# An expert loop with its gathers dealt one per expert, split TensorE signals, and routed rows collected in parts

## The chip, the cores and the metric

The kernel runs on one core of a Trainium2 chip. The metric is device time in microseconds (us), from one launch of the whole program. Engines are called by their profile names: PE is TensorE, ACT ScalarE, DVE VectorE, POOL GpSimd, SP the queue that issues most DMAs.

## What is computed

Four blocks in a row, each with a residual and a layer norm, on 2048 tokens of 128 values in fp32:

- causal linear attention with 16 heads of 8;
- a mixture of experts: a shared expert for all tokens, and 64 experts of width 384, of which each token takes its best 8 (weights renormalised over those 8);
- four encoder layers (linear attention, then a relu block of width 512), after `x * sqrt(128) + positions`;
- a routed block: the 75% of tokens with the highest scores go through `gelu(x @ w_block)`.

```python
h = jnp.einsum('ech,efh->ecf', buf, expert_w1)      # buf: each expert's tokens
x1, x2 = jnp.split(h, 2, axis=-1)
out = jnp.einsum('ecf,ehf->ech', x1 * jax.nn.silu(x2), expert_w2)
y = out[se, rank] * sw[:, None]                      # its gate
combined = jnp.zeros((T, H), x.dtype).at[st].add(y)
return shared_out + combined
```

## The kernel before

Five hand-ordered instruction streams, one for each engine, meet only in counting semaphores; no planner orders anything.

**Routing.** After the first attention the rows of x1 and the gates go to DRAM (`dispatch_rows`, 768 B a row). Experts are handled in 16 quads `Q` of `EG = 4`, experts `n = 4Q + j`. A quad has 5 blocks `b` of 128 slots, 160 slots for each of its experts. One-hot tables (`R["a"]`, `R["b"]`) multiplied on PE give the slot lists `gather_all` and `scatter_all`.

**The expert loop.** For expert `n` PE does: `expert_result(n - 2)` (L790, 3 products), then for `j` = 0 `turn_results(Q - 2, 1)`, for 1 and 2 `turn_inputs(Q + 1, j - 1)`, for 3 `turn_results(Q - 1, 0)` (the transposes L774 and L760), then `expert_hidden(n)` (L780, 6 products), which alone increments `expert_mm`. Each fp32 product has two matmul records. On `expert_mm >= n + 1` wait:

- ACT: `silu_of(n)` (L1153), then `keep_result(n - 2)` (L1157);
- DVE: `rows_back` (L1754) or `columns_of` (L1731), then `product(n)` (L1743), which also waits for the silu and which `expert_result(n)` waits for;
- SP: the next load of weights into a ring of 8 (576 KB an expert, L455);
- POOL: `step(n)`, its indirect DMAs. A gather (L1340) fetches 128 routed rows, a scatter (L1347) writes 128 weighted results to `returned_rows`. 30 gathers are issued ahead; then for each quad, from `n = 4Q + 8` on, at its four steps: 2 scatters, 3 scatters, 2 gathers, 3 gathers. The gathered rows have `GOT = 4` buffers.

**The way back.** When the last of 80 scatters has landed, SP reads `returned_rows` in 16 tiles of 512 KB (L467), in four groups `g` of 4 tiles. Meanwhile PE, ACT and DVE finish the shared expert of groups 2 and 3 (`late_hidden` L830 and L831, `late_product` L1791, `late_rows` L838, `add_base` L1787), all of it ahead of DVE's `collect`. `collect(g)` waits for all 4 tiles of its group; each tile is summed over its 8 rows per token in three halvings. `SUMMED = (3, 2, 0, 0)` is the number of tiles of each group that DVE sums (L1816, L1818); the others are POOL's (`sum_tiles`, L1469). Then the shared expert's rows are added (L1822), the norm taken (its rstd on POOL, L271), and `begin_state(0)`, `norm1` and the first layer's `turn_norm1` (L857) follow, one after the other.

Of the kernel before, what the change touches and what calls it, by code (L numbers as in the profile page):

```python
# [115 lines left out]
def program(nc, cst, xt0, xr0, l0w, l0p, l0r, bo0, l0s, ew, l1w, l1p, l1r, fin_r, mod_w, out):  # L116
    with ExitStack() as ctx:
# [27 lines left out]
        def carve(parts, at=0):  # L145

            made = {}
            for name, shape, dt in parts:
# [7 lines left out]
                elif len(shape) == 3:  # L156
# [48 lines left out]
        R = carve([("a", (TILES, NEG * RA * EG), F16), ("b", (2 * RB, TE), F16), ("mask", (TE,), F16)])  # L205
# [120 lines left out]
        SUMMED = (3, 2, 0, 0)  # L326
# [96 lines left out]
        def _(sp):  # L423
            sp.dma_start(w0[:, 0:W_O], l0w[:, 0:W_O]).then_inc(sem("first_in"), 16)
            sp.dma_start(cols(xt, 0), cols(xt0, 0)).then_inc(sem("first_in"), 16)
            sp.dma_start(l0ps[:], l0p).then_inc(sem("l0p_in"), 16)
            sp.dma_start(kv_bias[:], l0r.partition_broadcast(P)).then_inc(sem("l0p_in"), 16)
            sp.dma_start(C[:, 0:C_BLK], cst[:, 0:C_BLK]).then_inc(sem("first_consts_in"), 16)
            sp.dma_start(cols(xt, 1), cols(xt0, 1)).then_inc(sem("second_xt_in"), 16)
            sp.dma_start(w0[:, W_O:], l0w[:, W_O:]).then_inc(sem("wo_in"), 16)  # L430
            sp.dma_start(xr[:], xr0).then_inc(sem("xr_in"), 16)
            sp.dma_start(xt[:, 2 * GROUP:], xt0[:, 2 * GROUP:]).then_inc(sem("xt_in"), 16)
            sp.dma_start(sw[:], l0s).then_inc(sem("sw_in"), 16)
# [23 lines left out]
            sp.wait_ge(sem("expert_mm"), NE + LAG)  # L457
            sp.dma_start(w_qkv, l1w[0][:, 0:3 * P]).then_inc(sem("qkv_in"), 16)
            sp.dma_start(layer_cols[:], l1p).then_inc(sem("cols_in"), 16)
            sp.dma_start(lrows, l1r.rearrange("l a d -> l (a d)").partition_broadcast(P)).then_inc(sem("rows_in"), 16)  # L460
            sp.dma_start(w_o, l1w[0][:, 3 * P:4 * P]).then_inc(sem("o_in"), 16)
# [4 lines left out]
            for i in range(TILES):  # L466
                sp.dma_start(spare[i], mine[i]).then_inc(sem(f"returned_in{i // GT}"), 16)  # L467
            sp.dma_start(w_up, l1w[0][:, 4 * P:8 * P]).then_inc(sem("up_in"), 16)
            sp.dma_start(w_down, l1w[0][:, 8 * P:12 * P]).then_inc(sem("down_in"), 16)
            sp.dma_start(mod_sb, mod_w).then_inc(sem("mod_in"), 16)  # L470
            sp.dma_start(fin_rows, fin_r.rearrange("a d -> (a d)").partition_broadcast(P)).then_inc(sem("fin_in"), 16)

            with sp.Fori(1, LAYERS) as l:
                w = l1w[bass.ds(l, 1)].rearrange("a p n -> (a p) n")
                sp.wait_ge(sem("kv1_mm"), 2 * GROUPS * l)
                sp.dma_start(w_qkv, w[:, 0:3 * P]).then_inc(sem("qkv_in"), 16)
                sp.wait_ge(sem("out1_mm"), GROUPS * l)
                sp.dma_start(w_o, w[:, 3 * P:4 * P]).then_inc(sem("o_in"), 16)
                sp.wait_ge(sem("up_mm"), FFB * GROUPS * l)
                sp.dma_start(w_up, w[:, 4 * P:8 * P]).then_inc(sem("up_in"), 16)  # L480
                sp.wait_ge(sem("down_mm"), GROUPS * l)
                sp.dma_start(w_down, w[:, 8 * P:12 * P]).then_inc(sem("down_in"), 16)
# [6 lines left out]
        def _(pe):  # L489
# [4 lines left out]
            def project_first(g):  # L494
                if g == 1:
                    pe.wait_ge(sem("second_xt_in"), 16)
                if g == 2:
                    pe.wait_ge(sem("xt_in"), 16)
# [6 lines left out]
                pe.matmul(bank[0][:], w0[:, W_Q:W_Q + P], cols(xt, g), start=True, stop=True).then_inc(sem("q_mm"), 1)  # L505
# [82 lines left out]
            def attention_out(g, to):  # L588
                if g == 0:
                    pe.wait_ge(sem("wo_in"), 16)  # L590
# [22 lines left out]
            def route_logits(g):  # L613
                if g == 0:
                    pe.wait_ge(sem("sw_in"), 16)
# [106 lines left out]
            a16 = R["a"].rearrange("p i (g n) -> p i g n", n=RA * EG)  # L722
            b16 = R["b"].rearrange("p b (i e) -> p b i e", e=NE)

            def find_slots(call):
# [4 lines left out]
                for k, q in enumerate(FOUND[call]):  # L730
                    pe.wait_ge(sem("one_hots_ready"), 2 * q + 2)
                    for u in range(2):
                        at = 2 * RB * EG * (2 * k + u)
                        lo = EG * (2 * q + u)
                        for i in range(TILES):
                            mm = pe.matmul(slot_bank(call)[:, at:at + 2 * RB * EG], a16[:, i, 2 * q + u, :],
# [75 lines left out]
            turn_results(NEG - 2, 1).then_inc(sem("expert_mm"), 1)  # L812
            expert_result(NE - 1).then_inc(sem("expert_mm"), 1)
# [52 lines left out]
            def project(n, k, g, l):  # L866
                pe.wait_ge(sem("qkv_in"), 16 * (l + 1))
# [36 lines left out]
            def output(n, k, g, l):  # L904
                pe.wait_ge(sem("o_in"), 16 * (l + 1))
# [18 lines left out]
            def up(n, k, g, l):  # L924
                pe.wait_ge(sem("up_in"), 16 * (l + 1))
# [11 lines left out]
            def down(n, k, g, l):  # L937
                pe.wait_ge(sem("down_in"), 16 * (l + 1))
# [21 lines left out]
            def score(g):  # L960
                if g == 0:
                    pe.wait_ge(sem("mod_in"), 16)
                    pe.wait_ge(sem("mid_ready"), ITEMS)
                else:
# [3 lines left out]
                    sem("score_mm"), 1)  # L968
# [68 lines left out]
        def _(act):  # L1037
            def parts_of_q(g):
                act.wait_ge(sem("q_mm"), g + 1)
# [60 lines left out]
            act.wait_ge(sem("l0p_in"), 32)  # L1100
# [121 lines left out]
            def keep_scores(g):  # L1222
                if g >= 2:
                    act.wait_ge(sem("chosen"), g - 1)
                act.wait_ge(sem("score_mm"), g + 1)
# [66 lines left out]
        def _(pool):  # L1292
# [16 lines left out]
            def add_bias(g):  # L1309
                if g == 0:  # L1310
                    pool.wait_ge(sem("xr_in"), 16)
# [40 lines left out]
            AHEAD = 6  # L1352
# [725 lines left out]
```

## Time and profile before

| | us |
|---|---|
| median of 3 runs | 721.71 |
| lowest, highest | 721.12, 726.26 |
| the profiled execution | 723.01 |
| its span, first to last instruction | 721.2 |
| mean granted TensorE clock | 0.919 |

The profile is of one execution; times in it count from its first instruction. A row `start, us, engine line op out<-in xcount [idle <- releaser]` says that the engine sat idle that long before it, and what released it. Matmul ends are modelled. Idle time of an engine that is not the bottleneck costs nothing.

### The profile page before, as it was taken

Reading aid. Unit: us, or ns where it says so; the run is one execution under the profiler, and the core shown is the slowest. Engines: PE = TensorE matmul, PEld = TensorE weight load, DVE = VectorE, ACT = ScalarE, POOL = GpSimd, SP = SyncE. Lnnn points to the kernel's source line nnn. Section 1 sums busy time; section 2 is a strip of 40 time slices with the busy share of each in tenths; the row PEclk is TensorE's granted clock in tenths of the full one; section 3 lists DMA queues with packets and bytes.
Section 4 is the critical chain, followed back from the end, with each engine's and each line's share of the span. In section 5 each row is a group of like instructions: output and inputs, shape, how many; then the busy total and the mean of one; then the engine's idle time right before and its main releaser. Section 6 shows DMA issues by size and latency. Waiting matters only on the chain.

```text
span 721.2 us, 11097 instructions
## 1 busy us (share of the span) xinstructions
PE 580.0 (80%) x3755; PEld 479.8 (67%) x3755; DVE 453.1 (63%) x1362; ACT 230.2 (32%) x434; POOL 345.1 (48%) x341
## 2 busy tenths in 40 slices
PE   7998878668987787797999035789999999999960
PEld 5767655668977776797995024567787778778640
DVE  4678768943424322333433787887877787777994
ACT  3142234002322212222332011224344444443664
POOL 4656101873566666576444488343322332342352
PEclk9999997879999999999999556799999999999995
DMA  8960001126666766676716900000000000000001
GB/s 298 415 260 23 16 7 36 45 72 203 209 222 200 231 220 190 190 237 218 239 61 213 398 2 0 0 12 5 15 26 4 15 15 11 4 30 0 1 1 59
DMA packets 29564, 79.42 MB, mean 110 GB/s; under 512 B 7104, under 2 KB 12096, under 8 KB 29264
## 3 DMA queue, kind: packets, MB, share of 16 engines
q1 hardware_dynamic: 23088, 65.69, 26.3%
q0 software_dynamic: 6432, 13.16, 6.0%
q8 instruction: 25, 0.41, 0.2%
q14 instruction: 19, 0.16, 0.1%
HBM read 62.60 MB, written 16.25 MB: 109 GB/s over the span
## 4 chain that ended last, share of the span: by engine, by line
PE 58%; DVE 23%; issue 8%; another core or an unknown queue 4%; POOL 2%; ACT 2%; DMA 1%; SPq 0%; DVEq 0%; ACTq 0%; POOLq 0%
PE bank L780 13%; PE bank L946 6%; PE bank L790 6%; PE bank L934 6%; PE bank L539 4%; PE bank L876 3%; PE bank L894 2%; DVE stats L256 2%; DVE arena L1659 2%; PE bank L857 2%; PE bank L871 2%; DVE hidden L1743 2%; PE bank L885 2%; PE bank L912 2%
## 5 line engine op out<-in xcount | busy, mean ns | idle before, releaser
L271 POOL TENSOR_TENSOR rstd<-veps,minus_half 128x4 f32<-128x4 f32 x52 | 54.0, 1039 | 209.9 <-DVE veps L264 208.4
L780 PE MATMUL bank<-hidden,ring 128*128 128x160 f32 x768 | 123.4, 311 | 4.6 <-issue 2.7
L780 PEld LDWEIGHTS bank<-hidden,ring 128*128 128x128 f32 x768 | 113.4, 200 | 6.5 <-issue 4.3
L1347 POOL DMA_INDIRECT returned_rows<-x1t,scatter_all x80 | 79.3, 991 | 65.9 <-DVE x1t L1754 21.8
L1153 ACT ACTIVATE hidden<-bank 128x480 f32<-128x480 f32 x64 | 36.9, 576 | 177.6 <-PE bank L780 110.5
L790 PE MATMUL bank<-hidden,ring 128*128 128x160 f32 x384 | 66.4, 310 | 31.8 <-DVE hidden L1743 19.1
L790 PEld LDWEIGHTS bank<-hidden,ring 128*128 128x128 f32 x384 | 56.0, 193 | 37.3 <-DVE hidden L1743 22.8
L1731 DVE COPY hidden<-bank 128x384 f32<-128x384 f32 (+1 forms) x32 | 22.9, 719 | 66.3 <-PE bank L780 33.9
L1211 ACT ACTIVATE arena<-bank,layer_cols 128x512 f32<-128x512 f32 x64 | 44.0, 687 | 62.6 <-PE bank L934 62.6
L946 PE MATMUL bank<-ring,arena 128*128 128x128 f32 x512 | 59.9, 275 | 1.4 <-issue 1.4
L946 PEld LDWEIGHTS bank<-ring,arena 128*128 128x128 f32 x512 | 58.4, 192 | 2.4 <-issue 2.4
L1754 DVE TENSOR_TENSOR x1t<-bank,slot_gate 128x384 f32<-128x384 f32 (+1 forms) x32 | 15.6, 490 | 68.2 <-PE bank L780 52.6
L934 PE MATMUL bank<-arena,ring 128*128 128x512 f32 x128 | 57.6, 592 | 0.0
L857 PE MATMUL bank<-consts,arena 128*128 128x128 f32 x192 | 28.8, 285 | 26.3 <-DVE arena L295 26.2
L1743 DVE TENSOR_TENSOR hidden<-bank,hidden 128x480 f32<-128x480 f32 x64 | 41.7, 652 | 13.1 <-ACT hidden L1153 7.5
L295 DVE TENSOR_SCALAR arena<-shared,mv,rstd 128x128 f32<-128x128 f32 x128 | 38.1, 361 | 7.8 <-POOL rstd L271 7.8
L857 PEld LDWEIGHTS bank<-consts,arena 128*128 128x128 f32 x192 | 22.9, 145 | 29.9 <-DVE arena L295 24.0
L934 PEld LDWEIGHTS bank<-arena,ring 128*128 128x128 f32 x128 | 23.2, 190 | 23.4 <-issue 23.3
L1307 POOL TENSOR_TENSOR arena<-arena 128x512 f32<-128x512 f32 x30 | 32.7, 1122 | 12.5 <-DVE arena L1504 12.5
L539 PEld LDWEIGHTS bank<-consts,arena 128*128 128x128 f32 x256 | 31.8, 200 | 7.5 <-issue 4.2
L1513 DVE TENSOR_TENSOR arena<-bank,arena 128x512 f32<-128x512 f32 x36 | 24.4, 685 | 18.1 <-PE bank L539 12.2
L876 PEld LDWEIGHTS bank<-ring,arena 128*128 128x128 f32 x128 | 26.9, 210 | 13.0 <-issue 9.9
(222 smaller groups left out, 1156.9 us busy)
## 6 DMA issues: line engine op xcount, KB each, us to landing
ring<-in_ew SPq DMA_DIRECT2D x64, 576.0 KB
returned_rows<-zeros SPq DMA_DIRECT2D x16, 512.0 KB, 14.6
arena<-returned_rows SPq DMA_DIRECT2D x6, 512.0 KB, 12.7
hidden<-returned_rows SPq DMA_DIRECT2D x4, 512.0 KB, 5.0
ring<-returned_rows SPq DMA_DIRECT2D x4, 512.0 KB, 8.6
ring<-in_l1w SPq DMA_DIRECT2D x8, 256.0 KB, 2.6
returned_rows<-x1t,scatter_all POOLq DMA_INDIRECT x80
shared<-in_xr SPq DMA_DIRECT2D x1, 1024.0 KB, 8.3
```

Of the source, the lines that this page charges most:

```text
L271: pool.tensor_tensor(rstd[:, s, :], veps[:, s, :], minus_half[:], ALU.pow).then_inc(sem(f"rstd{which}_ready"), 1)
L295: ins = v.tensor_scalar(dst[:, i, :], src[:, i, :], mv[:, s, i, 0:1], rstd[:, s, i:i + 1], ALU.subtract, ALU.mult)
L539: mm = pe.matmul(bank[3 + c % 3][:, tile_of(t)], A["kvp"][:, g % 2, t, P * e:P * e + P], cum, start=True, stop=True)
L780: mm = pe.matmul(bank[2 * (n % 2) + part][:, CAP * f:CAP * f + CAP], ring[:, n % RING, P * (FB * part + f):P * (FB * part + f) + P], E["xt ...
L790: mm = pe.matmul(bank[4 + n % 2][:, 0:CAP], ring[:, n % RING, P * (2 * FB + f):P * (2 * FB + f) + P], E["prod"][:, n % 2, CAP * f:CAP * f ...
L857: mm = pe.transpose(bank[b][:, P * t:P * t + P], src[:, t, :], ident)
L876: mm = pe.matmul(bank[3 + h][:, 2 * D * t:2 * D * t + 2 * D], B["ht"][:, g, P * (2 * h + t):P * (2 * h + t) + P], w_qkv[:, P:3 * P], start ...
L934: pe.matmul(bank[(3, 4, 6, 7)[f]][:], w_up[:, P * f:P * f + P], B["ht"][:, g], start=True, stop=True).then_inc(sem("up_mm"), 1)
L946: mm = pe.matmul(bank[5][:, P * t:P * t + P], B["relu"][:, g % 2, f, P * t:P * t + P], w_down[:, P * f:P * f + P], start=(f == 0), stop=(f ...
L1211: act.activation(B["relu"][:, g % 2, f], bank[(3, 4, 6, 7)[f]][:], ACT.Relu, bias=layer_col(l, 5 + f)).then_inc(sem("relu_ready"), 1)
L1347: pool.indirect_dma_start(returned_dram[:, :], bass.IndirectOffsetOnAxis(ap=scatter_all[:, Q, b:b + 1], axis=0), E["back"][:, Q % BACK, b, ...
L1743: v.tensor_tensor(E["prod"][:, n % 2, :], bank[2 * (n % 2)][:, 0:FB * CAP], E["silu"][:, n % 2, :], ALU.mult).then_inc(sem("prod_g_ready"), 1)
```

## The change

Four things, and a renaming of semaphores (one serves first one transfer and later another, with the counts raised to match; PE's `project` waits for `16 * (l + 2)` instead of `16 * (l + 1)`, and so on) that frees some for new uses.

1. **Gathers and scatters.** The one-hot table `R["a"]` is laid out by quads, so that its first four quads become four more gather buffers (`GOT = 8`). 20 gathers are issued ahead of the loop, then 2 for each of experts 0 to 7, then 1 for each expert to 51; the scatters of a quad go 1, 1, 2, 1.
2. **Two signals.** PE increments `rows_mm` after `expert_result(n - 2)` and the turn, ahead of `expert_hidden(n)`; `expert_mm` stays behind `expert_hidden(n)`. ACT keeps result `n - 2` on `rows_mm`, ahead of its silu; DVE copies on `rows_mm` and multiplies when the silu is there.
3. **Return in parts.** DVE sums all of group 0 (`SUMMED = (4, 2, 0, 0)`), in parts of 2, 1 and 1 tiles, each when it has landed; POOL sums none of it.
4. **Later bases.** DVE's last two late products come behind its wait for the scatters, `add_base(2)` behind `collect(0)`, `add_base(3)` behind `norm_stats` of the first layer's norm; PE's first projection waits for both.

```diff
-        R = carve([("a", (TILES, NEG * RA * EG), F16), ...
+        R = carve([("a", (NEG, TILES, RA * EG), F16), ...
-        GOT, BACK = 4, 3
+        GOT, BACK = 8, 3
+        got_at += [arena[:, TILES * RA * EG // 2 * q:TILES * RA * EG // 2 * q + RB * ROUTED] for q in range(GOT - 4)]
...
-        SUMMED = (3, 2, 0, 0)
+        SUMMED = (4, 2, 0, 0)
+        PARTS = ((0, 2), (2, 1), (3, 1))
+
+        def returned_in(i):
+            return sem(f"returned_part{(0, 0, 1, 2)[i]}") if i < GT else sem(f"returned_in{i // GT}")
...
-            sp.wait_ge(sem("expert_mm"), NE + LAG)
+            sp.wait_ge(sem("rows_mm"), NE + LAG - 1)
...
             for n in range(NE):
                 Q, j = n // EG, n % EG
                 if n >= LAG:
-                    expert_result(n - LAG)
+                    done = expert_result(n - LAG)
+                if j == 0 and Q >= 2:
+                    done = turn_results(Q - 2, 1)
+                elif j in (1, 2) and Q < NEG - 1:
+                    done = turn_inputs(Q + 1, j - 1)
+                elif j == 3 and Q >= 1:
+                    done = turn_results(Q - 1, 0)
+                if n:
+                    done.then_inc(sem("rows_mm"), 1)
                 if j == 0:
-                    if Q >= 2:
-                        turn_results(Q - 2, 1)
                     pe.wait_ge(sem("xt_read"), 2 * (Q + 1))
-                elif j < 3 and Q < NEG - 1:
-                    turn_inputs(Q + 1, j - 1)
-                elif j == 3 and Q >= 1:
-                    turn_results(Q - 1, 0)
...
             def project(n, k, g, l):
+                if k == 0:
+                    pe.wait_ge(sem("base_ready"), GROUPS)
...
             for n in range(NE + LAG):
-                act.wait_ge(sem("expert_mm"), n + 1)
+                if n >= LAG:
+                    act.wait_ge(sem("rows_mm"), n)
+                    keep_result(n - LAG)
                 if n < NE:
+                    act.wait_ge(sem("expert_mm"), n + 1)
                     silu_of(n)
-                if n >= LAG:
-                    keep_result(n - LAG)
...
-            AHEAD = 6
+            BEFORE, FIRST_SCATTER = 4, 2 * EG
...
+            gather_blocks(0, BEFORE * RB)
             pool.wait_ge(sem("zeroed"), 16 * TOK * TOPK // (8 * P))
+            for n in range(NE + LAG):
+                if n < NE:
+                    pool.wait_ge(sem("expert_mm"), n + 1)
+                else:
+                    pool.wait_ge(sem("rows_mm"), n)
+                if n < FIRST_SCATTER:
+                    gather_blocks(BEFORE * RB + 2 * n, 2)
+                else:
+                    Q = (n - FIRST_SCATTER) // EG
+                    gathering = BEFORE * RB + FIRST_SCATTER + n < NEG * RB
+                    for b in (((0,), (1,), (2, 3), (4,)) if gathering else ((0, 1), (2, 3), (4,), ()))[n % EG]:
+                        scatter_block(Q, b)
+                    gather_blocks(BEFORE * RB + FIRST_SCATTER + n, 1)
...
             for n in range(NE):
                 Q, j = n // EG, n % EG
-                v.wait_ge(sem("expert_mm"), n + 1)
+                if n:
+                    v.wait_ge(sem("rows_mm"), n)
...
             def collect(g):
-                v.wait_ge(sem(f"returned_in{g}"), 16 * GT)
-                count = SUMMED[g]
...
+                if g == 0:
+                    for first, count in PARTS:
+                        v.wait_ge(returned_in(first), 16 * count)
+                        k = add_rows(g, first, count)
```

## Rows read from the trace of the kernel before

**Rows 1.** Busy time by stretch: expert loop (three), scatters' end, first layers.

```profile
152.00:184.00 32.00, 27.41 (x173) 26.65 (x174) 10.33 (x23) 7.35 (x16) 14.25 (x16) 0.87 0.52 161
184.00:334.00 150.00, 121.84 (x834) 116.02 (x833) 49.74 (x101) 36.07 (x81) 97.76 (x101) 0.97 0.66 213
343.00:376.00 33.00, 32.41 (x244) 32.18 (x242) 14.48 (x28) 11.69 (x26) 14.73 (x15) 1.00 0.50 157
404.00:476.00 72.00, 34.64 (x131) 25.97 (x132) 58.50 (x173) 13.05 (x18) 47.03 (x48) 0.67 0.15 58
```

**Rows 2.** Timeline, two neighbouring experts late in the loop.

```profile
356.81 1.80 PE L780 MATMUL bank<-hidden,ring 128*128 128x160 f32 x12
358.65 0.57 ACT L1153 ACTIVATE hidden<-bank 128x480 f32<-128x480 f32 x1 [1.85 <-PE bank L780]
359.48 1.80 PE L780 MATMUL bank<-hidden,ring 128*128 128x160 f32 x12
```

**Rows 3.** Timeline, one quad of the middle, in order of time.

```profile
277.28 0.82 DVE L1731 COPY hidden<-bank 128x384 f32<-128x384 f32 x1 [3.18 <-PE bank L780]
277.95 0.64 DVE L1743 TENSOR_TENSOR hidden<-bank,hidden 128x480 f32<-128x480 f32 x1
278.02 0.98 POOL L1347 DMA_INDIRECT returned_rows<-x1t,scatter_all  x1 [2.08 <-PE bank L780]
279.30 0.98 POOL L1347 DMA_INDIRECT returned_rows<-x1t,scatter_all  x1 [0.30 <-issue]
282.56 1.80 PE L780 MATMUL bank<-hidden,ring 128*128 128x160 f32 x12
285.33 1.80 PE L780 MATMUL bank<-hidden,ring 128*128 128x160 f32 x12
286.97 0.95 POOL L1340 DMA_INDIRECT arena<-dispatch_rows,gather_all  x1 [0.30 <-issue]
288.04 0.57 ACT L1153 ACTIVATE hidden<-bank 128x480 f32<-128x480 f32 x1 [5.39 <-PE bank L780]
288.64 0.66 DVE L1743 TENSOR_TENSOR hidden<-bank,hidden 128x480 f32<-128x480 f32 x1 [0.18 <-issue]
288.81 1.01 POOL L1347 DMA_INDIRECT returned_rows<-x1t,scatter_all  x1 [0.90 <-PE bank L780]
289.36 1.27 PE L790 MATMUL bank<-hidden,ring 128*128 128x160 f32 x6 [2.23 <-issue]
292.49 0.57 ACT L1153 ACTIVATE hidden<-bank 128x480 f32<-128x480 f32 x1 [3.53 <-remote]
293.23 0.98 POOL L1347 DMA_INDIRECT returned_rows<-x1t,scatter_all  x1 [2.10 <-remote]
```

**Rows 4.** Timeline of POOL, start of the loop.

```profile
173.94 0.94 POOL L1340 DMA_INDIRECT logits<-dispatch_rows,gather_all  x1 [0.30 <-issue]
184.03 1.02 POOL L1347 DMA_INDIRECT returned_rows<-x1t,scatter_all  x1 [9.15 <-DVE x1t L1754]
```

**Rows 5.** Timeline, from the last scatter to the first norm of the sum.

```profile
387.98 0.98 POOL L1347 DMA_INDIRECT returned_rows<-x1t,scatter_all  x1 [0.30 <-issue]
390.24 1.76 SPq L467 DMA_DIRECT2D hidden<-returned_rows  x4
397.27 0.69 DVE L1787 TENSOR_TENSOR shared<-bank,x 128x512 f32<-128x512 f32 x1 [3.04 <-PE bank L838]
398.00 3.72 POOL L1469 TENSOR_TENSOR hidden<-hidden 128x512 f32<-128x512 f32 x2 [9.04 <-DMA hidden<-returned_rows]
403.30 0.69 DVE L1822 TENSOR_TENSOR arena<-arena,shared 128x512 f32<-128x512 f32 x1
406.78 1.12 DVE L295 TENSOR_SCALAR x<-arena,mv,rstd 128x128 f32<-128x128 f32 x4 [1.15 <-POOL rstd L271]
```

**Rows 6.** The tile hidden from 376 to 400 us: DVE's first halving, and the landings.

```profile
L1816 DVE TENSOR_TENSOR hidden<-hidden x1: 2697/2697/2697, 398.4 to 398.4; 128x1536 f32<-128x1536 f32 x1
DMA to landing us min/median/max: 3.6/5.0/6.3
```

More of the change, by code:

```diff
@@ L504, in project_first @@
                     pe.wait_ge(sem("logits_ready"), g - 2)
-                pe.matmul(bank[0][:], w0[:, W_Q:W_Q + P], cols(xt, g), start=True, stop=True).then_inc(sem("q_mm"), 1)
+                pe.matmul(bank[0][:], w0[:, W_Q:W_Q + P], cols(xt, g), start=True, stop=True).then_inc(sem("q_mm_then_score_mm"), 1)
                 for h in range(2):
@@ L811, in _ @@
             expert_result(NE - 2)
[L812 to L813 removed]
+            turn_results(NEG - 2, 1).then_inc(sem("rows_mm"), 1)
+            expert_result(NE - 1).then_inc(sem("rows_mm"), 1)
             for c in range(2):
@@ L1350, in scatter_block, with gather_blocks @@
                                         oob_is_err=False).then_inc(sem(f"scattered{Q % BACK}"), 16)
[L1352 removed]
+            BEFORE, FIRST_SCATTER = 4, 2 * EG
+            def gather_blocks(first, count):
+                for k in range(first, min(first + count, NEG * RB)):
+                    gather_block(k // RB, k % RB)
             pool.wait_ge(sem("rows_out"), 16 * 2 * GROUPS)
[L1354 to L1356 removed]
+            gather_blocks(0, BEFORE * RB)
             pool.wait_ge(sem("zeroed"), 16 * TOK * TOPK // (8 * P))
[L1358 to L1375 removed]
+            for n in range(NE + LAG):
[11 more added lines that the diff above has]
+                    gather_blocks(BEFORE * RB + FIRST_SCATTER + n, 1)
+            scatter_block(NEG - 2, RB - 1)
+            for b in range(RB):
+                scatter_block(NEG - 1, b)
             def row_of(l, k):
@@ L1459, in sum_tiles @@
             def sum_tiles(g):
+                if SUMMED[g] == GT:
+                    return
                 pool.wait_ge(sem(f"returned_in{g}"), 16 * GT)
@@ L1658, in low_table @@
                 n = last - first
-                ins = v.tensor_tensor(a_out[:, first:last, Q],
+                ins = v.tensor_tensor(a_out[:, Q, first:last],
                                       a_in[:, first:last, EG * Q:EG * Q + EG].unsqueeze(2).to_broadcast([P, n, RA, EG]),
@@ L1773, in _ @@
                     gates_of(Q + 1)
-            v.wait_ge(sem("expert_mm"), NE + 1)
+            v.wait_ge(sem("rows_mm"), NE)
             rows_back(NEG - 2, 1)
@@ L1797, in _ @@
                 late_product(m)
-            add_base(SOON)
-            for m in range(FB * SOON + 4, FB * GROUPS):
-                late_product(m)
-            add_base(SOON + 1)
             v.wait_ge(sem("consts_in"), 16)
@@ L1808, in _, with add_rows @@
             blk = C[:, C_BLK:C_BLK + P]
-            def collect(g):
-                v.wait_ge(sem(f"returned_in{g}"), 16 * GT)
-                count = SUMMED[g]
-                if count:
-                    rows = spare_rows(g, 0, count)
-                    for width in (4 * D, 2 * D):
-                        ch.after(ch.did(v.tensor_tensor(rows[:, :, 0:width], rows[:, :, 0:width],
-                                                        rows[:, :, width:2 * width], ALU.add)))
-                    k = ch.did(v.tensor_tensor(H[:, g, 0:count, :], rows[:, :, 0:D], rows[:, :, D:2 * D], ALU.add))
+            def add_rows(g, first, count):
+                rows = spare_rows(g, first, count)
+                for width in (4 * D, 2 * D):
+                    ch.after(ch.did(v.tensor_tensor(rows[:, :, 0:width], rows[:, :, 0:width],
+                                                    rows[:, :, width:2 * width], ALU.add)))
+                return ch.did(v.tensor_tensor(H[:, g, first:first + count, :], rows[:, :, 0:D], rows[:, :, D:2 * D], ALU.add))
+            def collect(g):
+                if g == 0:
+                    for first, count in PARTS:
+                        v.wait_ge(returned_in(first), 16 * count)
+                        k = add_rows(g, first, count)
+                else:
+                    v.wait_ge(sem(f"returned_in{g}"), 16 * GT)
+                    if SUMMED[g]:
+                        k = add_rows(g, 0, SUMMED[g])
+                if SUMMED[g]:
                     ch.after(k)
-                v.wait_ge(sem("pool_sums"), 3 * sum(GT - n for n in SUMMED[:g + 1]))
+                if SUMMED[g] < GT:
+                    v.wait_ge(sem("pool_sums"), 3 * sum(GT - n for n in SUMMED[:g + 1]))
                 v.wait_ge(sem("base_ready"), g + 1)
@@ L2021, in _ @@
             ch.after(ch.did(v.tensor_scalar(lrows[:, :, 0:D], lrows[:, :, 0:D], 1.0, None, ALU.add)))
+            for m in range(FB * SOON + 4, FB * GROUPS):
+                late_product(m)
             steps = GROUPS * (2 * 2 * GT + 1 + 3)
```

102 lines of the change are left out of this document (43 added, 59 removed).

## The prediction

> **What bounds the kernel now.** I read the busy time by stretch first. Late in the expert loop, 343 to 376 us, PE is busy 32.4 of 33 us; in the middle, 184 to 334 us, 121.8 of 150 [rows 1]. An expert has 18 matmul records of its own and on average 2.5 transposes, 20.5 in all. So the late stretch does 244/20.5 = 11.9 experts at 2.77 us each, which is PE's own pace, and the middle 834/20.5 = 40.7 experts at 3.69 us. That is 0.92 us an expert that PE does not need, 37 us over the middle, in a loop that everything after it waits for.
>
> Then the timeline, to see what PE waits for. In the late stretch the silu starts at 358.65, when the products of 356.81 + 1.80 have just ended [rows 2]. In the middle it does not. The products of 282.56 end by their records at 284.36, and ACT starts its silu at 288.04, 3.7 us late; those of 285.33 end at 287.13 and the silu starts at 292.49, 5.4 us late [rows 3]. DVE, SP and POOL, which wait for the same `expert_mm`, start with ACT to within 0.1 us where they have nothing else to wait for: POOL's wait of 2.10 us ends at 293.23, behind that same signal and its set-up. The count arrives late. PE then sits idle 2.23 us before the result product at 289.36 [rows 3].
>
> What stands beside it is POOL. From 278.02 to 293.23 it issues the quad's 10 indirect DMAs, 1.29 us from one start to the next (279.30 less 278.02), and the two pauses in that time exceed the usual 0.30 by 0.6 and 1.8 us [rows 3]: 12.9 + 2.4 = 15.3 us for four experts, of which PE needs 11.1. In the late stretch POOL has 15 such DMAs in 33 us and no gathers, and the signals come on time [rows 1, 2]. So the loop's middle goes at POOL's pace, by way of signals that come late while POOL issues without a break. Why a signal is held is not in the trace.
>
> Last the way back. The last scatter is issued at 387.98, SP reads from 390.24 on, the fourth tile lands at 397.9 and DVE's addition of the base starts at 403.30 [rows 5, 6]. Nothing of the first layer can start before it.
>
> **Gathers and scatters.** The change does not take a DMA away; it moves them. From expert 8 to 51 POOL now has 44 gathers and 55 scatters, 9 for four experts instead of 10. Before, 101 of POOL's instructions in 150 us took 101 x 1.29 = 130.3 us, and 19.7 us were pauses, for ten quads 2.0 us each [rows 1, 3]. After, eleven quads take 99 x 1.29 = 127.7 us, and if pauses stay at 2.0 us a quad, 21.7 more: 149.4 us. Before, the same 44 experts took 40.7 in 150 us and 3.3 at 2.77: 159.1 us. The difference is **-9.7 us**, the term I take for this part. Its bounds are far apart. From below: all signals on time, PE at 2.77 us, 44 x 2.77 = 121.9 us, -37. From above: a pause after every expert, 9 x 1.29 + 4 x 1.2 = 16.4 us a quad (1.2 is half of the 2.4 above), 180.5 us, +21. I take the middle value since it is the same rule, 10 DMAs and two pauses, read on 9.
>
> Experts 0 to 7: before, 173/20.5 = 8.4 experts took 32 us, 8.7 more than at 2.77 [rows 1]; POOL finished its 30 gathers at 174.9 and then sat idle for 9.15 us [rows 4], in which the signals were on time. After, it issues 2 x 1.25 us in every 2.77 us and that rest is gone, but so are the five in a row. I take 0, with -7 and +5 as bounds (the excess gone; five clean experts at the middle's 0.92 us more). Gathers run 28 blocks ahead of the expert number and are needed at 5 blocks a quad, so the last, issued at expert 51, is needed at 57: no wait of PE for rows. Scatters of a quad are all out by n = 4Q + 11, and DVE needs the buffer again at 4Q + 19.
>
> The table's new layout has the same elements in each instruction; 0, and the find-slots products read the same 128 columns.
>
> **Two signals.** When a signal comes late, DVE copies 384 columns for 0.82 us ahead of the product, and the product starts 0.67 us behind the copy's start; where the copy is the shorter one it starts 0.60 us behind, which is the silu's 0.57 [rows 3]. With the copy done during the hidden products, 0.07 to 0.15 us are saved at each expert whose product PE waits for, some 15 in the middle: **-1.0**, bounds -3 and 0. Where PE never waits this is worth nothing. What is queued behind ACT's new wait is the silu; ACT waits for the count of a turn that is ahead of the hidden products on PE, so it cannot be the later of the two. The 63 added increments I price at 0, since the product that carries them is not lengthened in any row; but they are 63 more signals of the kind that come late, and that belongs to the slow rival.
>
> A rule speaks against this part. The Trainium skill, in TensorE: Matmul & The Clock Gate, under the cost of the per-tile semaphore tail, says that increments serialize, with a fit of 26.3 ns each; as an estimate from that page, 65 of them would add 1.7 us. No row here shows the cost of one, and the sum does without it.
>
> **Return in parts.** SP's first read is issued at 390.24; the landings take 3.6 us for the first and 6.3 for the fourth, which was issued last, at about 391.6 [rows 5, 6]. So tiles land near 393.9, 395.3, 396.6 and 397.9. DVE used to start at 398.4 with 1536 columns, for 2.70 us; 512 columns take 0.69 us elsewhere (L1822), so 1536 should take 3 x 0.53 + 0.16 = 1.75 [rows 5, 6]. POOL was summing beside it for 3.72 us [rows 5], and now it does not. Part 0 takes 1.23 + 0.69 + 0.42 and gaps, 2.4 us, from 395.3 to 397.7; parts 1 and 2 take 0.69 + 0.42 + 0.29 + 0.1 = 1.5 each, to 399.2 and 400.7. The addition of the base then starts at 400.8 instead of 403.30: **-2.5**, bounds 0 (each step at the slower rate of 2.70/1.75, part 2 done at 403.0) and -3.5. On this the skill agrees with the row: SBUF — State Buffer, under who interferes with whom, says that a DVE instruction with two SBUF inputs contends with a GpSimd instruction that reads SBUF.
>
> The moved work: `late_product` 10 and 11 are behind the wait for the scatters, which ends near 390.3, and their silus come later than that anyway; before, DVE's last base addition ran at 397.27, only 0.4 us ahead of the collecting [rows 5]. It and its twin now take 0.69 us each in DVE's waits for a rstd, of which the first is 1.15 us long [rows 5], and the second alike. If that cover were gone they would cost 1.4 us. PE's new wait for the bases is behind `h1_ready`, which comes later on DVE. The first layers, 404 to 476 us, are DVE's (58.5 of 72 us busy [rows 1]) and shift as a whole.
>
> **The sum.** -9.7 - 1.0 - 2.5 = -13.2. The profiled execution took 723.0 us, 1.3 above the median, so 709.8 on its scale and **708.5** on the median's. A difference of 1%, 7.2 us, is about what the measurement of this kernel can tell from none.
>
> **The rivals.**
> - Signals on time throughout (0.22). Gathers no longer come five in a row, and scatters alone in runs of five hardly delay a signal [rows 2]. Then -37 and up to -7 for the loop and -2.5: between 675 and 685. Against it: POOL still issues 9 x 1.29 = 11.6 us in PE's 11.1, without a break.
> - The deal changes nothing (0.20): each gather costs what it costs, wherever it stands. Then only the return's 2.5 and the copy's 1.0: 718.
> - More pauses, slower (0.15). A late signal is let through when POOL has run out of permitted work; with a small portion at each step, POOL runs out at every expert, and each time all engines wait. At x pauses of 1.2 us a quad costs 11.6 + 1.2x; it breaks even with 14.5 at x = 2.4, and at four the loop loses 21 us: 723 + 21 - 3.5 - 1.3 = 739. The two signals for each expert speak for it, the on-time signals of the late stretch, with five scatters in a run, against.
> - The forecast (0.43), 700 to 716 by its own bounds.
>
> **Range and chances.** 680 takes in most of the first rival, 729 the milder half of the slow one; outside are the strongest forms of both. Faster by over 1%: 0.36 + 0.22 + 0.04 = 0.62. Within: 0.05 + 0.16 + 0.03 = 0.24. Slower: 0.14.
>
> **What would show it.** Right: 184 to 334 us holds about 900 matmul records instead of 834, POOL's DMAs still 1.29 us apart, fewer waits over 3 us of ACT for L780, base addition some 2.5 us closer to the last scatter. Wrong: as many late silus per quad as before (second rival), one late silu for each expert and POOL pauses near 2 us after every step (third), or no late silu and PE busy over 95% (first). A DVE wait for the second base, or PE waiting for gathered rows, would break terms that I set to 0.

## The result and the profile after

| us | before | after |
|---|---|---|
| median (4 runs each) | 721.41 | 711.5 |
| span of the profiled execution | 721.2 | 709.9 |
| mean granted TensorE clock | 0.919 | 0.920 |

The ratio is 0.9843, 95% interval 0.9801 to 0.9886: 1.6% faster. By the two spans the change took 11.3 us off. First the busy time by stretch of the kernel after, the same stretches as [rows 1].

```profile
152.00:184.00 32.00, 28.50 (x186) 27.73 (x186) 10.18 (x23) 7.96 (x17) 19.68 (x21) 0.89 0.55 179
184.00:334.00 150.00, 128.51 (x896) 124.06 (x895) 55.48 (x112) 42.22 (x89) 97.54 (x98) 0.97 0.69 226
343.00:376.00 33.00, 30.69 (x199) 26.91 (x200) 14.30 (x28) 11.58 (x24) 17.89 (x18) 1.00 0.47 147
404.00:476.00 72.00, 43.51 (x202) 33.06 (x201) 59.89 (x172) 17.66 (x25) 44.39 (x48) 0.76 0.03 11
```

The middle, 184 to 334 us, holds 896 matmul records where before had 834, and 98 POOL instructions where it had 101: more experts for about as many DMAs. To see where the 11.3 us lie I take both traces apart at events that both have: the first product of experts 0, 8 and 52, the last scatter, the first product of the first layer (PE's `turn_norm1`) and the end.

```
us                                before    after   difference
to the start of expert 0          152.97   153.16     +0.2
experts 0 to 7                     28.38    26.50     -1.9
experts 8 to 51                   161.81   151.06    -10.8
expert 52 to the last scatter      44.82    48.20     +3.4
last scatter to turn_norm1         24.88    22.23     -2.7
turn_norm1 to the end             308.34   308.73     +0.4
```

Next the timeline of the kernel after, one quad of the middle, to hold against [rows 3].

```profile
288.05 0.99 POOL L1358 DMA_INDIRECT returned_rows<-x1t,scatter_all  x1 [0.30 <-issue]
289.34 0.99 POOL L1351 DMA_INDIRECT arena<-dispatch_rows,gather_all  x1 [0.30 <-issue]
289.61 1.80 PE L786 MATMUL bank<-hidden,ring 128*128 128x160 f32 x12
290.63 1.01 POOL L1358 DMA_INDIRECT returned_rows<-x1t,scatter_all  x1 [0.30 <-issue]
291.94 0.99 POOL L1351 DMA_INDIRECT arena<-dispatch_rows,gather_all  x1 [0.30 <-issue]
294.31 0.57 ACT L1163 ACTIVATE hidden<-bank 128x480 f32<-128x480 f32 x1 [0.38 <-remote]
294.91 0.66 DVE L1757 TENSOR_TENSOR hidden<-bank,hidden 128x480 f32<-128x480 f32 x1 [1.02 <-ACT hidden L1163]
295.05 1.00 POOL L1358 DMA_INDIRECT returned_rows<-x1t,scatter_all  x1 [2.12 <-PE bank L786]
295.62 1.08 PE L796 MATMUL bank<-hidden,ring 128*128 128x160 f32 x6 [1.02 <-DVE hidden L1757]
```

The signals still come late: the products of 289.61 end by their records at 291.41, and ACT's silu starts at 294.31, 2.9 us late. POOL still issues at 1.29 to 1.31 us and then stands for 2.12 us. Of the 44 experts 22 have a silu over 1 us late, 24 before. What has changed is the number of DMAs: 98 from the start of expert 8 to that of expert 52, where before has 105, with pauses that add up to about as much.

The 3.4 us that were given back lie where before had no late signals at all. The last gather now goes out at expert 53 (expert 49 in before), and POOL issues from 329.0 to 340.6 almost without a break, nine DMAs, of which these are the last six:

```profile
332.91 1.01 POOL L1358 DMA_INDIRECT returned_rows<-x1t,scatter_all  x1 [0.30 <-issue]
334.22 0.99 POOL L1351 DMA_INDIRECT arena<-dispatch_rows,gather_all  x1 [0.30 <-issue]
335.51 1.00 POOL L1358 DMA_INDIRECT returned_rows<-x1t,scatter_all  x1 [0.30 <-issue]
336.17 1.80 PE L786 MATMUL bank<-hidden,ring 128*128 128x160 f32 x12
336.82 0.99 POOL L1358 DMA_INDIRECT returned_rows<-x1t,scatter_all  x1 [0.30 <-issue]
338.37 0.98 POOL L1358 DMA_INDIRECT returned_rows<-x1t,scatter_all  x1 [0.56 <-issue]
338.94 1.08 PE L796 MATMUL bank<-hidden,ring 128*128 128x160 f32 x6 [0.98 <-issue]
339.65 0.98 POOL L1358 DMA_INDIRECT returned_rows<-x1t,scatter_all  x1 [0.30 <-issue]
342.21 0.61 ACT L1163 ACTIVATE hidden<-bank 128x480 f32<-128x480 f32 x1
343.57 1.08 PE L796 MATMUL bank<-hidden,ring 128*128 128x160 f32 x6 [1.08 <-DVE hidden L1757]
```

The silu of the products that end at 337.97 starts at 342.21, 4.2 us late. Experts 54 and 55 take 4.03 and 4.52 us here, where before takes 2.77 and 2.67. From expert 52 on, up to its wait ahead of the last result product, PE stands idle for 2.3 us in all, and in before not at all.

Last the way back, the timeline of the kernel after against [rows 5], and the landings from the tile `hidden` against [rows 6].

```profile
378.92 0.98 POOL L1358 DMA_INDIRECT returned_rows<-x1t,scatter_all  x1 [0.30 <-issue]
386.25 1.95 DVE L1824 TENSOR_TENSOR hidden<-hidden 128x1024 f32<-128x1024 f32 x2 [1.07 <-DMA hidden<-returned_rows]
388.23 0.43 DVE L1826 TENSOR_TENSOR arena<-hidden 128x256 f32<-128x256 f32 x1
391.47 0.69 DVE L1842 TENSOR_TENSOR arena<-arena,shared 128x512 f32<-128x512 f32 x1
393.70 0.68 DVE L1802 TENSOR_TENSOR shared<-bank,x 128x512 f32<-128x512 f32 x1
395.31 1.11 DVE L296 TENSOR_SCALAR x<-arena,mv,rstd 128x128 f32<-128x128 f32 x4 [0.93 <-POOL rstd L272]
DMA to landing us min/median/max: 3.8/5.4/7.0
```

From the last scatter to the addition of the base it takes 391.47 - 378.92 = 12.55 us, where before took 15.32. The moved `add_base` (L1802) runs at 393.70 and DVE still waits 0.93 us for the rstd behind it.

### The profile page after: what moved, and what is told of

The parts are those of the page before. It is cut to its first block, busy times and chain, and to the rows that moved or that the text cites. A ratio compares the mean times of both kernels' runs of the same rounds, so it can differ in the third digit from the quotient of the medians.

```text
span 709.9 us, 11093 instructions
## 1 busy us (share of the span) xinstructions
PE 576.3 (81%) x3755; PEld 478.2 (67%) x3755; DVE 453.5 (64%) x1368; ACT 233.6 (33%) x434; POOL 342.1 (48%) x338
## 4 chain that ended last, share of the span: by engine, by line
PE 58%; DVE 19%; issue 10%; another core or an unknown queue 5%; ACT 3%; POOL 3%; DMA 1%; SPq 0%; DVEq 0%; ACTq 0%; POOLq 0%
PE bank L786 11%; PE bank L956 7%; PE bank L796 6%; PE bank L944 6%; PE bank L545 4%; PE bank L886 3%; PE bank L904 2%; DVE stats L257 2%; PE bank L865 2%; ACT hidden L1163 2%; PE bank L879 2%; DVE hidden L1757 2%; PE bank L895 2%; PE bank L922 2%
## 5 line engine op out<-in xcount | busy, mean ns | idle before, releaser
L786 PE MATMUL bank<-hidden,ring 128*128 128x160 f32 x768 | 121.5, 309 | 3.4 <-DVE hidden L1745 2.5
L796 PE MATMUL bank<-hidden,ring 128*128 128x160 f32 x384 | 66.4, 310 | 26.2 <-DVE hidden L1757 21.4
L1351 POOL DMA_INDIRECT arena<-dispatch_rows,gather_all x50 | 53.7, 1075 | 35.9 <-DVE scatter_all L1704 16.6
L956 PEld LDWEIGHTS bank<-ring,arena 128*128 128x128 f32 x512 | 58.4, 192 | 2.4 <-issue 2.4
L1167 ACT ACTIVATE hidden<-bank 128x160 f32<-128x160 f32 x64 | 29.4, 460 | 60.2 <-PE bank L766 30.9
L865 PE MATMUL bank<-consts,arena 128*128 128x128 f32 x192 | 28.6, 285 | 23.6 <-DVE arena L296 23.5
L944 PEld LDWEIGHTS bank<-arena,ring 128*128 128x128 f32 x128 | 23.2, 190 | 23.4 <-issue 23.3
L545 PE MATMUL bank<-consts,arena 128*128 128x128 f32 x256 | 34.5, 288 | 0.0
```

Of the source, the lines that this page charges most:

```text
L545: mm = pe.matmul(bank[3 + c % 3][:, tile_of(t)], A["kvp"][:, g % 2, t, P * e:P * e + P], cum, start=True, stop=True)
L786: mm = pe.matmul(bank[2 * (n % 2) + part][:, CAP * f:CAP * f + CAP], ring[:, n % RING, P * (FB * part + f):P * (FB * part + f) + P], E["xt ...
L796: mm = pe.matmul(bank[4 + n % 2][:, 0:CAP], ring[:, n % RING, P * (2 * FB + f):P * (2 * FB + f) + P], E["prod"][:, n % 2, CAP * f:CAP * f ...
L865: mm = pe.transpose(bank[b][:, P * t:P * t + P], src[:, t, :], ident)
L944: pe.matmul(bank[(3, 4, 6, 7)[f]][:], w_up[:, P * f:P * f + P], B["ht"][:, g], start=True, stop=True).then_inc(sem("up_mm"), 1)
L956: mm = pe.matmul(bank[5][:, P * t:P * t + P], B["relu"][:, g % 2, f, P * t:P * t + P], w_down[:, P * f:P * f + P], start=(f == 0), stop=(f ...
```

## The experiments

Twelve runs of ten kernels, on four chips. Each kernel ran beside runs of the kernel before on the same chip, and its ratio is to those; the profile of before is always that of the first comparison, whose chip is not on record. "Late" is the time from the end of an expert's hidden products, by their records, to its silu.

**One part at a time.** Three kernels keep the new names of the semaphores and one part of the change each.

> The kernel after with only part 1 left (table by quads, 8 gather buffers, the new deal of gathers and scatters); one signal for each expert, the way back and the base additions as before. Theory A (the deal made the gain in the loop): the middle loses about the 9.7 us of the prediction, and the kernel comes out at 711 to 714. Theory B (the second signal made it, since ACT and DVE do their copies ahead of a late signal): 718 to 722. The return's part, 2 to 2.5 us, is missing here under both.

> The kernel after with only part 2 left (rows_mm ahead of the expert's first products, expert_mm behind them); the old deal with 4 gather buffers, the old way back. Theory A: -1.0 us, between 719 and 722, with as many late silus as before. Theory B: 710 to 714. A third possibility, that 63 more signals of the kind that come late delay the others more: over 723.

> The kernel before with parts 3 and 4 (group 0 summed by DVE in three parts, the last two late products and the last two base additions moved). Theory A: the addition of the base to group 0 starts some 2.5 us sooner after the last scatter, and the kernel takes 718.5 to 720. Rival: another group or the wait for both bases is next, and less than 1 us remains, 720.5 to 722.

Measured, on one chip where before took 725.2: part 1 alone 714.1, ratio 0.9836 (0.980 to 0.9872); part 2 alone 725.6, ratio 1.0006 (0.9977 to 1.0036); parts 3 and 4 alone 721.5, ratio 0.995 (0.992 to 0.9981). Theory A holds and B falls: the gain is the deal's, some 3 us are the return's, and the second signal gives nothing that these runs can tell. (The whole change did not run beside its parts on this chip, so that they add up is not shown.) In the profile of part 1 alone, experts 8 to 51 take 150.0 us, as in the kernel after.

The profile of part 1 alone also shows what the way back costs without parts 3 and 4:

```profile
389.54 3.69 DVE L1822 TENSOR_TENSOR hidden<-hidden 128x1536 f32<-128x1536 f32 x2
389.68 4.13 POOL L1478 TENSOR_TENSOR hidden<-hidden 128x512 f32<-128x512 f32 x2 [9.62 <-DMA hidden<-returned_rows]
394.63 0.69 DVE L1835 TENSOR_TENSOR arena<-arena,shared 128x512 f32<-128x512 f32 x1 [0.40 <-POOL arena L1478]
```

Beside POOL, DVE's two halvings add 1536 and 768 columns in 3.69 us, 1.60 ns a column; alone, 1024 and 512 in 1.95 us, 1.27 ns. From the last scatter (379.07) to the base addition 15.6 us pass here. Over all profiles it is 15.3 to 16.0 us without parts 3 and 4 (before and two kernels) and with them 12.5 to 12.8 in ten profiles and 13.8 in one, two_each_b.

**Two DMAs at each expert.**

```diff
...
-                    gather_blocks(BEFORE * RB + FIRST_SCATTER + n, 1)
...
+                for _ in range(2):
+                    g_due = EG * (got_n // RB) - 9 if got_n < NEG * RB else 999
+                    p_due = EG * (put_n // RB) + 2 * EG + 6
...
+                    if g_can and (g_due <= p_due or not p_can):
+                        gather_block(got_n // RB, got_n % RB)
+                        got_n += 1
+                    elif p_can:
+                        scatter_block(put_n // RB, put_n % RB)
+                        put_n += 1
...
```

> The kernel after, but POOL issues exactly two indirect DMAs at each expert (2.6 us of its time in PE's 2.7 to 2.8) instead of 2, 2, 3 and 2, and goes on with two an expert to the end of the loop, whichever of gather or scatter is due first. Theory A1 (a signal comes late because POOL has issued some six DMAs without a break, which three in one expert bring about): most late silus go, an expert costs about 2.8 us, and the kernel takes 680 to 695. Theory A2 (what counts is how many DMAs POOL has in flight over tens of us, whatever the breaks of 0.2 us): the silus stay late as in the kernel after and the kernel takes 708 to 715.

Measured on the same chip: 704.6, ratio 0.9706 (0.967 to 0.9742), 2.9% faster than before and some 9 us faster than part 1 alone. It lies between the ranges of the two theories, and A1's reason falls: 18 silus of experts 8 to 51 are still over 1 us late. An expert takes 3.08 us from 8 to 51, since only 88 DMAs are issued in that time instead of 98; part of it comes back later, 58.8 us from expert 52 to the last scatter instead of 48.2, since the last scatter now goes out 14.9 us after the start of the last record of the last result product instead of 11.1, and PE waits 2.43 us for the last quad's rows, ahead of expert 57.

**Another chip.** The next four runs were meant to part the count of DMAs from their mixing. no_signals is the kernel after with the one signal of before; the portions of the other two, for the four experts of a quad, are these:

```diff
-  after:        scatters (0,), (1,), (2, 3), (4,)      and 1, 1, 1, 1 gathers
+  deal_bursts:  scatters (0, 1), (2, 3, 4), (), ()     and 0, 0, 2, 2 gathers
+  even_ten:     scatters (0,), (1, 2), (3,), (4,)      and 1, 1, 1, 2 gathers (BEFORE = 6)
```

> The changed kernel once more, as the yardstick for the three beside it: about 11 us less than before, as in the first comparison, which had a ratio of 0.984.

> The kernel after without part 2: one signal for each expert again, ACT and DVE wait for it alone; the even deal and the way back in parts stay. By the prediction's term 1 us slower than the kernel after, within 0 to 3. The rival, that the second signal is worth nothing or costs something (alone it gave 1.0006 of before): no slower, or faster by up to 1.7 us.

> The kernel after with the same 9 DMAs in a quad of experts, 20 gathers ahead and 2 at each of experts 0 to 7, but from expert 8 to 51 dealt in runs of one kind as before: 2 scatters, 3 scatters, 2 gathers, 2 gathers. Theory A (9 instead of 10 in a quad is what counts, as the prediction's sum has it): as the kernel after, within 3 us. Theory B (the mixing and the even portions count): the middle goes back towards 3.7 us an expert and the kernel loses most of 10 us.

> The kernel after with before's 10 DMAs in a quad (30 gathers ahead, none at experts 0 to 7), but mixed: scatter and gather; two scatters and a gather; scatter and gather; scatter and two gathers. Theory A (the count): 10 x 1.29 us and two pauses of 1.2 us make 15.3 us a quad as before, so about 9 us slower than the kernel after. Theory B (the mixing): within 3 us of the kernel after.

On this chip before takes 677.8 us, 43 to 47 less than on the others, at about the same granted clock (0.92 against 0.91 to 0.92). Ratios: the kernel after 0.9976 (0.9958 to 0.9994), without the signals 0.9987 (0.997 to 1.0004), in runs of one kind 0.994 (0.9921 to 0.9959), mixed tens 0.9994 (0.998 to 1.0008). So the change is worth a quarter of a per cent here. The kernel after, by stretch and in its timeline:

```profile
184.00:294.00 110.00, 110.00 (x831) 110.00 (x830) 49.84 (x100) 41.88 (x81) 84.18 (x85) 1.00 0.90 281
...
293.47 0.57 ACT L1163 ACTIVATE hidden<-bank 128x480 f32<-128x480 f32 x1 [1.17 <-PE bank L786]
294.10 0.98 POOL L1351 DMA_INDIRECT arena<-dispatch_rows,gather_all  x1 [0.31 <-issue]
295.38 1.00 POOL L1358 DMA_INDIRECT returned_rows<-x1t,scatter_all  x1 [0.30 <-DVE x1t L1768]
...
310.73 0.55 PE L766 MATMUL bank<-consts,arena 128*128 128x128 f32 x3 [2.94 <-DMA arena<-dispatch_rows,gather_all]
```

PE is busy 110.00 of 110 us. The silu of 293.47 follows products that start at 291.63 and take 1.79, 0.05 us behind them; none of the 64 is over 1 us late. POOL issues 85 DMAs in 110 us, one each 1.29, with no pause at all. So POOL's issuing without a break does not by itself hold PE's signals; it does so on some chips. The two profiles of the kernel after differ by 36.0 us, of which 35.6 lie in experts 0 to 51, where the late signals are. What is left is POOL's own pace: 9 DMAs take 11.6 us and PE's quad 10.9, POOL falls behind, and PE waits 2.94 us for gathered rows at 310.73, ahead of expert 57. All four kernels give the same 2.72 us an expert from 8 to 51; they differ behind it (47.1 to 51.4 us from expert 52 to the last scatter), and even_ten sends its last scatter 2.4 us later than the kernel after (345.0 against 342.6).

**Count or mixing, again.** Two of these kernels were run once more.

> The same kernel as deal_bursts, in the hope of a chip that holds signals back. There, theory A (the count of 9 in a quad): within 3 us of the kernel after, a ratio near 0.984. Theory B (mixing, even portions): a ratio near 0.995 to 1. On a chip without late signals: 0.994 again.

> The same kernel as even_ten. On a chip that holds signals back, theory A (the count): 10 DMAs in a quad take what they took before, 3.6 to 3.75 us an expert from 8 to 51, and the whole differs from before only by the way back, a ratio of 0.993 to 0.998. Theory B (mixing alone helps): 0.985 or less. On a chip without late signals: 0.999 again.

Both met chips that hold signals, one each. Nine DMAs in runs of one kind: 708.0, ratio 0.9811 (0.9792 to 0.9831), so not slower than the even deal. Ten DMAs, mixed: 728.2, ratio 1.01 (1.007 to 1.0129), and from expert 8 to 51 it takes 162.5 us, before 161.8. It is the count; mixing brings nothing. (The ratio 1.01 lies outside what either theory foresaw; the stretch from 8 to 51, 3.69 us an expert, is what theory A foresaw. Dealt in runs it is even a little cheaper: one DMA takes 1.291 us from start to start there and 1.309 in the kernel after, on the chip without late signals 1.285 and 1.299.) That even_ten_2 ends above before, way back in parts and all, comes in the main from its start, 36.4 us for experts 0 to 7. The first four rows are of even_ten_2, the last is of before:

```profile
157.95 1.80 PE L786 MATMUL bank<-hidden,ring 128*128 128x160 f32 x12
167.38 0.95 POOL L1351 DMA_INDIRECT arena<-dispatch_rows,gather_all  x1 [0.30 <-issue]
168.63 0.95 POOL L1351 DMA_INDIRECT arena<-dispatch_rows,gather_all  x1 [0.30 <-issue]
172.71 0.57 ACT L1163 ACTIVATE hidden<-bank 128x480 f32<-128x480 f32 x1 [6.60 <-remote]
...
168.95 0.94 POOL L1340 DMA_INDIRECT logits<-dispatch_rows,gather_all  x1 [4.37 <-DVE slot_gate L1739]
```

The products end at 159.75 and their silu starts at 172.71, 13.0 us late, 3.1 us after the end of the last of the 30 gathers. The last 17 of them go out without a break, and that sets even_ten_2 apart: with its 8 gather buffers none of the 30 waits for one. With 4 buffers the 26th waits for a buffer to come free, 4.37 us in before. The first eight experts take 27.1, 28.4 and 30.6 us in the three profiles with 30 gathers ahead and 4 buffers, and 36.4 in this one with 8; in the five with 20 ahead and two at each expert they take 26.0 to 26.6. (On the chip without late signals even_ten's take 22.2.)

**Without the weight loads.**

```diff
-            for n in range(RING, NE):
-                sp.wait_ge(sem("expert_mm"), n - RING + LAG + 1)
-                sp.dma_start(ring[:, n % RING, :], ew[n]).then_inc(...)
-                pe.wait_ge(sem(f"expert_in{n % RING}"), 16 * (n // RING + 1))
+                pe.wait_ge(sem(f"expert_in{n % RING}"), 16)
```

> The kernel after without the 56 loads of expert weights behind the first ring of 8: experts 8 to 63 compute with the weights of the first eight. It takes 95% of the loop's bytes away and leaves POOL's DMAs and all counts as they are. On a chip that holds signals back, theory P (a signal is held by POOL's issuing): the late silus stay, some 27 over 1 us, 3.4 us an expert, 705 to 712. Theory D (it is held by the traffic of all DMAs together): the late silus go, 2.75 us an expert, 670 to 682. On a chip without late signals it says nothing and takes what the kernel after takes there, near 675.

Measured: 707.9, ratio 0.9813 (0.9776 to 0.9849), about what the kernel after has. The stretch, and one late silu of its timeline:

```profile
184.00:334.00 150.00, 128.25 (x914) 123.06 (x913) 54.82 (x109) 42.09 (x87) 99.03 (x100) 0.99 0.18 54
...
278.34 1.80 PE L782 MATMUL bank<-hidden,ring 128*128 128x160 f32 x12
284.08 0.57 ACT L1159 ACTIVATE hidden<-bank 128x480 f32<-128x480 f32 x1 [1.04 <-PE bank L782]
```

The DMA engines are busy 0.18 of the time instead of 0.69 and move 54 GB/s instead of 226, and the silu is 3.9 us late all the same; 20 of 44 are over 1 us late. Of the two, theory P holds: it is not the bytes of the weight loads. The traffic of the indirect DMAs themselves is still there, so whether their issuing or their transfers hold the signal is not parted. (The expectation's 95% was too much: 226 to 54 is 76%.)

**The best version.**

```diff
-                for _ in range(2):
+                for _ in range(3 if n < FIRST_SCATTER and n % 2 else 2):
```

> The kernel of two DMAs at each expert, with three at experts 1, 3, 5 and 7, so that the gathers end at expert 52 and PE does not wait for the last quad's rows at expert 57, which cost 2.5 us there. If the chip is one that holds PE's signals back (before takes about 722 there): 700 to 704. If it is one that does not (before takes about 678 there): theory A1 would have no signals left to free, so what remains is POOL's own pace and the last quad's rows: 671 to 675, against 675.9 for the kernel after.

Measured, on a chip that holds signals (before 722.1): 702.3, ratio 0.9735 (0.9715 to 0.9754), the fastest beside two_each. PE's wait for rows is gone and the last scatter follows the last result by 10.4 us again, but the first eight experts take 28.8 us instead of 26.5, so it is no better than two_each. Neither two_each nor two_each_b ran on the other kind of chip.

**All profiles in one table.** From the start of expert 8 to that of expert 52; a pause is what an interval between two of POOL's DMAs that starts in the stretch has over 1.29 us, where it is longer than 1.6. The last four ran on the chip without late signals.

```
kernel          DMAs     us   us/DMA   pauses us   late >1 us
before           105   161.8   1.541      26.3        24
even_ten_2       105   162.5   1.547      25.6        24
p2_signals       105   164.0   1.562      28.2        22
p34_return       105   165.7   1.578      31.7        22
after             98   151.1   1.541      23.7        22
p1_deal           98   150.0   1.530      22.6        21
deal_bursts_2     98   148.1   1.512      21.4        24
no_loads          98   148.2   1.512      19.2        20
two_each_b        90   136.9   1.521      22.6        16
two_each          88   135.5   1.540      24.0        18
after_again       92   119.7   1.301       0           0
no_signals        92   119.7   1.301       0           0
deal_bursts       94   119.7   1.273       0           0
even_ten          90   119.7   1.330       0           0
```

(The profiled execution of p34_return took 728.9 us, 1% over its median. In six rows a pause runs over the end of the stretch; without it they have 23.0 in before, 21.4 in even_ten_2, 23.4 in p2_signals, 22.7 in p34_return, 21.6 in two_each_b and 22.9 in two_each, much as the others.) On the chips that hold signals a DMA of POOL costs 1.51 to 1.58 us of the loop, however they are dealt.

## Why the prediction was right

**The middle.** The term was -9.7 us: 9 DMAs for four experts instead of 10, at 1.29 us, with pauses as before. Measured -10.8. The rule behind it, DMAs times their pace plus pauses, holds in its parts: 98 DMAs (99 foreseen) at 1.309 us instead of 1.29, pauses 23.7 us (21.7 foreseen). Before has 105 DMAs in the same stretch, since its experts 48 to 51 have only the five scatters: seven fewer, at 1.54 us each in both, are the 10.8 us. deal_bursts_2 and even_ten_2 show that the count is the cause, and the table that the us for each DMA hardly move from 88 to 105 of them.

**Experts 0 to 7.** I took 0 within -7 and +5; measured -1.9. The sign that I left open is that of the gathers ahead of the loop: 27.1 to 30.6 us with 30 of them and 4 buffers, 36.4 with 30 and 8, about 26 with 20.

**The end of the loop.** Here a term was missing. The prediction had all experts from 52 on clean in both kernels, and said of the gathers only that PE does not wait for them. They now end four experts later, in a run with scatters, and +3.4 us come from the late signals there. On the chip without late signals the same stretch costs as much, 48.3 us in after_again, for another reason: PE's wait of 2.94 us for gathered rows, which the prediction had excluded. I had priced what the deal does to the stretch that it relieves and not where the moved DMAs end.

**Two signals.** -1.0 within -3 and 0. Not seen; this term was put too high. The product of a late expert starts 0.60 us behind its silu (median) in the kernel after and 0.67 in before, but 0.61 in p34_return, which has no second signal either; p2_signals gives 1.0006 within 0.3%, and no_signals 0.9987 where after_again has 0.9976. A reading that fits, and that no run shows, is that the loop goes at POOL's pace and PE gives back at the next late signal what it saves ahead of a product. In p2_signals one silu (of expert 46) starts 8.3 us behind its products, which end at 318.61, later than any in before, and no run tells whether the second signal has to do with it. The estimate of 1.7 us that the Trainium skill's rule on increments gave (TensorE: Matmul & The Clock Gate, the cost of the per-tile semaphore tail) lies inside p2_signals' interval of 2 us to either side, so no run here shows or excludes it.

**Return in parts.** -2.5; measured -2.8 at the base addition. The step values held: the first halving starts 7.33 us after the last scatter (7.3 foreseen), part 0's two halvings take 1.95 us (1.92 foreseen), the base addition starts 12.55 us after the scatter (12.8 foreseen).

**Later bases.** 0, and DVE's wait for the rstd behind the first of them is still 0.93 us long. Not quite 0, though: POOL starts this rstd 0.62 us after the start of DVE's last step before it (L265) and in before 0.25 us, so the norm is applied 3.84 us after the base addition instead of 3.48. By the first layer's turn 0.1 us of it is left.

**The sum.** -13.2 foreseen; by the same two profiles -11.3, by the medians -9.9. Between -13.2 and -11.3 stand the end of the loop, +3.4, the rest of the layers and the time ahead of the loop, +0.6, and the start, -1.9. It was luck that the start, which I had put at 0, took back over half of the end, and that the middle gave 1.1 us more than foreseen while the second signal's 1.0 did not come.

**The rivals.** Signals on time throughout: not on this chip, but it is how the fourth chip runs, where the time of before, 677.8 us, says the same of before, so that the change wins little by it. No change from the deal: excluded by p1_deal. More pauses: pauses for 44 experts are 23.7 us, against 23.0 or 26.3 in before, as one counts; the second signal adds none. That a held signal comes through when POOL has run out of work, on which this rival rested, is borne out by even_ten_2's 13 us and by the kernel after, where 21 of all 27 late silus start while POOL stands; but POOL waits for the same signal, and in before some also came through during the 30 gathers, so it is not the whole rule.

**The signs.** The 896 matmul records, the 1.3 us between DMAs and the base addition came as named. Two other signs tell nothing. ACT's waits of over 3 us ahead of a silu fell from 25 to 12, as the forecast has it, but p2_signals, which gains nothing, has 8 of them: with the second signal ACT waits in two steps. And the late silus of experts 8 to 51 stayed at 22 against 24, which was to be the sign that the deal changes nothing; p1_deal has 21 of them and takes 11 us less than before.

## What stays open

Why a signal of PE is held is not settled. Shown: it is held on three chips and not on a fourth, though before ran on all four; the five scatters in a run of [rows 2]'s stretch hold nothing, while late silus stand beside runs of 7 to 10 of POOL's indirect DMAs in before's middle and of 17 in even_ten_2; their number sets the loss, and neither their order nor the bytes of the weight loads do. Long runs of scatters alone were not tried. Each chip was visited once, so whether this belongs to the chip or to its state at that time is open too, and before has a profile on none of the four. ACT's and DVE's own signals are not held: in the late experts of the kernel after, DVE's product follows the silu after 0.60 us (median), as in the others, and PE's result product follows DVE's after 0.71 (in the others PE is still at work, and it is 1.97). That the path in question belongs to PE alone is argued from this, not shown. Which part of the chip differs was not tried.

## What to carry to other kernels

Count an engine's instructions for each turn of the loop before looking at their order: where one engine issues without a break, taking one of ten away was worth 11 us and reordering them nothing. When work is moved out of a stretch, price the stretch where it ends too; 3.4 us were given back there. And run a kernel on more than one chip before trusting a gain that comes from late signals: the same change gave 1.6% in the first comparison and 0.24% on the chip without them.

## What the runs showed of the hardware

Two chips differed by 6% on one program, at about the same granted clock (before: 677.8 against 721 to 725 us). In the kernel after, profiled on both kinds, the difference is the time at which PE's increments are seen while POOL issues indirect DMAs: 0.05 us behind the products on one. On the others it is up to 5.4 us in the middle of before, 8.3 once in p2_signals, and 13.0 us in even_ten_2 beside 17 gathers without a break. And POOL's indirect DMAs of 128 rows cost 14 to 18 ns more each when gathers and scatters alternate than in runs of one kind (1.299 against 1.285 us on the chip without late signals, 1.309 against 1.291 in profiles from chips with them).
